# Layer-norm arithmetic of two attentions moved from VectorE to GpSimd, and the side work placed at other heads

## The reference, cut to what matters

```python
ln_out = layernorm(x, ln_s, ln_b)          # (x - m) * rsqrt(v + EPS) * scale + bias
q, k, v = projections                       # self: all of ln_out; cross: k, v of encoder_states
scores = einsum('bhqd,bhkd->bhqk', q, k) / sqrt(HD)      # 16 heads of 32 channels
scores = scores * mask - 10000.0 * (1.0 - mask)
ctx = merge_heads(softmax(scores) @ v)
x = x + ctx @ w_o + b_o
```

## Time and profile before

| what | value |
|---|---|
| median of 3 runs | 4261.32 us (4250.41, 4262.61, 4261.32) |
| profiled execution | 4252.74 us, its span 4250.9 us |
| mean granted TensorE clock | 0.954 of full speed |
| busy, share of the span | PE 88%, DVE 71%, PEld 68%, ACT 48%, POOL 41% |

### The profile page before, as it was taken

The page is one execution under the profiler, slowest core; times in us unless marked ns, Lnnn a source line. Parts: engine busy times, 40 slices in busy tenths (PEclk is TensorE's granted clock), DMA queues, the critical chain, the costliest instruction groups (busy, mean ns, idle before and its releaser), DMA issues. The chain is left out here.

```text
span 4250.9 us, 71399 instructions
## 1 busy us (share of the span) xinstructions
PE 3730.4 (88%) x21636; PEld 2882.3 (68%) x21636; DVE 2998.0 (71%) x6732; ACT 2057.8 (48%) x5384; POOL 1742.2 (41%) x1210
## 2 busy tenths in 40 slices
PE   5998998588888886999999778999999999999976
PEld 4777777477777774899999655666666666666643
DVE  5777777477777775556556338888888878888872
ACT  4777777367777675545545322333333333333322
POOL 2444444144444441000000135666666666666652
PEclk9999999799999997999999889999999999999988
DMA  3434434344444443010010210000000000000000
GB/s 110 104 99 109 104 99 104 96 116 118 104 114 110 122 104 116 30 44 30 30 41 33 73 50 18 24 24 23 24 23 24 23 24 23 24 23 23 23 18 15
DMA packets 146611, 256.58 MB, mean 60 GB/s; under 512 B 27184, under 2 KB 32048, under 8 KB 145424
## 3 DMA queue, kind: packets, MB, share of 16 engines
q1 hardware_dynamic: 146448, 254.49, 22.0%
HBM read 107.62 MB, written 33.55 MB: 33 GB/s over the span
## 5 line engine op out<-in xcount | busy, mean ns | idle before, releaser
L1201 POOL TENSOR_TENSOR c_S<-c_S,c_rT 128x1024 f32<-128x1024 f32 x256 | 558.1, 2180 | 458.4 <-DVE c_S L1479 417.6
L1479 DVE TENSOR_TENSOR_SCAN c_S<-c_wT,c_s,c_vb 128x256 f32<-128x256 f32 x1024 | 709.0, 734 | 45.0 <-issue 2.7
L1474 DVE TENSOR_TENSOR c_vb<-c_kT,c_vb 128x512 f32<-128x512 f32 x512 | 352.4, 688 | 286.4 <-PE c_vb L1645 255.6
L348 POOL TENSOR_TENSOR x_prob<-x_prob,x_rsums 128x512 f32<-128x512 f32 x256 | 275.2, 1075 | 477.7 <-DVE x_rsums L510 477.7
L348 POOL TENSOR_TENSOR s_prob<-s_prob,s_rsums 128x512 f32<-128x512 f32 x256 | 275.2, 1075 | 431.0 <-DVE s_rsums L510 431.0
L1645 PE MATMUL c_vb<-c_vhl,c_spread 128*128 128x512 f32 x512 | 300.4, 597 | 73.6 <-DVE c_S L1479 60.6
L404 ACT ACTIVATE x_prob<-x_t,x_tmin 128x256 f32<-128x256 f32 x512 | 256.4, 502 | 218.3 <-DVE x_tmin L503 218.0
L404 ACT ACTIVATE s_prob<-s_t,s_tmin 128x256 f32<-128x256 f32 x512 | 256.5, 502 | 193.9 <-DVE s_tmin L503 193.6
L862 PE MATMUL b_ps<-b_ln_high,b_w_high 128*128 128x256 f32 x1024 | 290.9, 284 | 14.8 <-DVE b_ln_low L804 14.8
L863 PE MATMUL b_ps<-b_ln_low,b_w_high 128*128 128x256 f32 x1024 | 290.8, 284 | 0.0
L864 PE MATMUL b_ps<-b_ln_high,b_w_low 128*128 128x256 f32 x1024 | 290.8, 284 | 0.0
(11 more groups left out here) (266 smaller groups left out, 10572.4 us busy)
## 6 DMA issues: line engine op xcount, KB each, us to landing
s_stack<-s_parts_qk SPq DMA_DIRECT2D x384, 128.0 KB, 2.4
x_stack<-x_parts_qk SPq DMA_DIRECT2D x384, 128.0 KB, 2.4
s_x_in<-in_x SPq DMA_DIRECT2D x16, 512.0 KB, 3.6
s_xb<-in_x SPq DMA_DIRECT2D x16, 512.0 KB, 4.1
x<-s_x_out SPq DMA_DIRECT2D x16, 512.0 KB, 4.8
x_enc<-in_ctx SPq DMA_DIRECT2D x16, 512.0 KB, 4.4
x_x_in<-x SPq DMA_DIRECT2D x16, 512.0 KB, 3.7
x_xb<-x SPq DMA_DIRECT2D x16, 512.0 KB, 4.1
```

The source lines that it names most:

```text
L348: nc.gpsimd.tensor_tensor(prob[:, h % 4, :, :], prob[:, h % 4, :, :], rsums[:, h, :].unsqueeze(2).to_broadcast([P, TC, T]), ALU.mult).then ...
L1201: nc.gpsimd.tensor_tensor(S[:, n % 4, :, 0:T], S[:, n % 4, :, 0:T], rT[:, par, :, :], ALU.mult).then_inc(z_ready, 1)
L1474: nc.vector.tensor_tensor(pair(vb, i), pair(kT[:, par, :, :], i), pair(vb, i), ALU.mult)
L1479: op = nc.vector.tensor_tensor_scan(S[:, n % 4, c, 1:T + 1], wT[:, par, c, :], vb[:, c, :], s0[:, par, c, n:n + 1], ALU.mult, ALU.add)
```

## The change: what it does

It does four things in both attentions, and nothing in the other two phases.

1. POOL, no longer DVE, forms the normed input: two TENSOR_SCALAR instructions of 128x512 behind the power, at head 3 instead of head 6. DVE's statistics move from head 4 to head 3.
2. POOL, no longer DVE, forms the low parts of lnT0 and lnT1, at head 7 (self) or 6 (cross), behind its product of the head before.
3. The addition to `xb` on POOL moves from head 1 to head 2 (self) or 3 (cross).
4. The side work on PE, ACT and DVE stands at other heads, with one table for each attention.

```diff
@@ -131,9 +131,12 @@
     LT = 3
 
 
-    FILLS = {0: ["k2", "ctx2"], 1: ["q3"], 2: ["k3"], 4: ["ctx3"], 5: ["v0"],
-             6: ["v1"] + (["encT0", "encT1"] if cross else []), 7: ["lnT0", "lnT1", "out0"], 8: ["out1", "ctx0"],
-             9: ["q0"], 10: ["k0"], 11: ["q1"], 12: ["k1", "ctx1"], 15: ["q2"]}
+    SELF_FILLS = {0: ["q3"], 1: ["k2"], 3: ["k3"], 4: ["ctx2", "ctx3", "v0"], 6: ["v1", "lnT0", "lnT1"], 7: ["out0"], 8: ["out1", "ctx0"], 9: ["q0"], 10: ["k0"], 11: ["q1", "k1"], 12: ["ctx1"], 13: ["q2"]}
+    SELF_AT = {"xb": 2, "root": 3, "stats": 3, "low": 7}
+    CROSS_FILLS = {1: ["q3", "k2"], 2: ["ctx2"], 3: ["k3", "ctx3", "v0"], 4: ["v1", "lnT0"], 5: ["encT0", "lnT1"], 6: ["out0"], 7: ["out1"], 8: ["encT1"], 9: ["ctx0", "q0"], 10: ["k0"], 11: ["q1"], 12: ["k1"], 13: ["ctx1", "q2"]}
+    CROSS_AT = {"xb": 3, "root": 3, "stats": 3, "low": 6}
+
+    FILLS, AT = (CROSS_FILLS, CROSS_AT) if cross else (SELF_FILLS, SELF_AT)
     PART = {"attn": ("k2", "q3", "k3", "v0", "v1", "ctx0", "ctx1"), "lag": ("ctx2", "ctx3", "out0", "out1"),
             "front": ("encT0", "encT1", "lnT0", "lnT1", "q0", "k0", "q1", "k1", "q2")}
     PART_OF = {name: part for part, names in PART.items() for name in names}
@@ -195,7 +198,7 @@
         mask_released = sem("mask_released")
         filled = sem("filled")
         emptied = {"act": sem("emptied_act"), "dve": sem("emptied_dve")}
-        stats_ready, rstd_ready, xhat_ready = sem("stats_ready"), sem("rstd_ready"), sem("xhat_ready")
+        stats_ready, xhat_ready = sem("stats_ready"), sem("xhat_ready")
         xb_ready, out_ready = sem("xb_ready"), sem("out_ready")
         weights_loaded = [sem("weights_loaded_0"), sem("weights_loaded_1")]
         weight_high, weight_split = sem("weight_high"), sem("weight_split")
@@ -337,7 +340,7 @@
 
                 def body(k, parts):
                     for n in range(NH):
-                        if n == 1 and "lag" in parts:
+                        if n == AT["xb"] and "lag" in parts:
                             pool.wait_ge(xb_loaded, 16 * k)
                             nc.gpsimd.tensor_tensor(xb[:, :, :], xb[:, :, :],
                                                     row_out[:, :].unsqueeze(1).to_broadcast([P, TC, C]),
@@ -348,10 +351,19 @@
                             nc.gpsimd.tensor_tensor(prob[:, h % 4, :, :], prob[:, h % 4, :, :],
                                                     rsums[:, h, :].unsqueeze(2).to_broadcast([P, TC, T]),
                                                     ALU.mult).then_inc(prob_ready, 1)
-                        if n == 5 and "front" in parts:
+                        if n == AT["root"] and "front" in parts:
                             pool.wait_ge(stats_ready, k + 2)
-                            nc.gpsimd.tensor_tensor(rstd[:, :], ve[:, :], w["neghalf"][:, :],
-                                                    ALU.pow).then_inc(rstd_ready, 1)
+                            nc.gpsimd.tensor_tensor(rstd[:, :], ve[:, :], w["neghalf"][:, :], ALU.pow)
+                            nc.gpsimd.drain()
+                            for tc in range(TC):
+                                op = nc.gpsimd.tensor_scalar(x_in[:, tc, :], x_in[:, tc, :], mv[:, tc, 0:1],
+                                                             rstd[:, tc:tc + 1], ALU.subtract, ALU.mult)
+                            op.then_inc(xhat_ready, 1)
+                        if n == AT["low"] and "front" in parts:
+                            for i in range(2):
+                                pool.wait_ge(emptied["act"], units.emptied(k + 1, f"lnT{i}"))
+                                high, low = [x[:, 2 * i:2 * i + 2, :] for x in ln_parts]
+                                nc.gpsimd.tensor_tensor(low, lnT[:, 2 * i:2 * i + 2, :], high, ALU.subtract).then_inc(ln_split, 1)
 
                 iterations(pool, body)
 
@@ -447,7 +459,7 @@
 
                 def move(k, name, parts):
 
-                    if name in ("v0", "v1"):
+                    if name in ("v0", "v1", "lnT0", "lnT1"):
                         return
                     if PART_OF[name] not in parts:
                         if units.reader(name) == "dve":
@@ -456,11 +468,7 @@
                         return
                     i = int(name[-1])
                     u = ps[:, units.unit(name), :]
-                    if name[:-1] == "lnT":
-                        dve.wait_ge(emptied["act"], units.emptied(k + 1, name))
-                        high, low = [x[:, 2 * i:2 * i + 2, :] for x in ln_parts]
-                        nc.vector.tensor_tensor(low, lnT[:, 2 * i:2 * i + 2, :], high, ALU.subtract).then_inc(ln_split, 1)
-                    elif name[:-1] == "encT":
+                    if name[:-1] == "encT":
                         dve.wait_ge(high_ready, high_done(k, name))
                         high, low = [x[:, 2 * i:2 * i + 2, :] for x in src_parts]
                         nc.vector.tensor_tensor(low, u.rearrange("p (a n) -> p a n", a=2), high,
@@ -508,12 +516,9 @@
                         if ("lag" if n < 1 else "attn") in parts:
                             dve.wait_ge(exp_done, head(kk, h))
                             nc.vector.reciprocal(rsums[:, h, :], psums[:, h, :]).then_inc(rsum_ready, 1)
-                        if n == 4 and "front" in parts:
+                        if n == AT["stats"] and "front" in parts:
                             dve.wait_ge(x_loaded, 16 * k + 32)
                             layernorm_stats(nc, x_in, stats, mv, ve).then_inc(stats_ready, 1)
-                        if n == 6 and "front" in parts:
-                            dve.wait_ge(rstd_ready, k + 2)
-                            layernorm_apply(nc, x_in, mv, rstd, x_in).then_inc(xhat_ready, 1)
                         for name in FILLS.get(n - 1, []):
                             move(k, name, parts)
                     for name in FILLS.get(NH - 1, []):
```

## The result

| | before | after |
|---|---|---|
| median of 12 runs | 4260.73 us (4250.41 to 4271.32) | 4278.57 us (4269.41 to 4283.99) |
| profiled execution's span | 4250.9 us | 4279.8 us |
| ratio after / before | | 1.0041, 95% interval 1.0029 to 1.0053 |

What follows compares the result with a forecast made beforehand. Neither PE nor DVE was full; they took turns waiting for each other. Cross -22, self -5 and the front bodies +4 made -23 us on 4252.7, 4230, given as 4232 us; range 4190 to 4266.

Steps and rivals of the forecast that it cites:

- part 2, "work onto POOL": POOL's new TENSOR_SCALARs: 1.05 us each between bounds of 0.25 and 2.1, adding 4.2 us a turn.
- the 0.3 us wait at head 6: Self: POOL's product of head 3 comes 0.3 us late for PE's transposes at head 6.
- Rival D: POOL becomes the late one if its TENSOR_SCALAR takes 2.1 us: +45 on -23, about 4275 us; chance 0.06.
- the thin stretch: Cross heads 14, 15 and 0 without side work: some 7 us with PE at about a third, then a lower clock.
- the late product: Self: POOL's product of head 3 held up behind the normed input, 0.3 us in the turn's sum.
- the walk: Head-by-head sum of the new order's turn before clock losses: cross 45.8 us, self 44.9 us.
- The stack DMAs were late at heads 0 and 1: Cross: the first stack slots may be 1 us late at heads 0 and 1, where PE can spare it.
- removing 4 us from DVE is worth nothing by itself in self: Heads 6 and 8: DVE waits for PE there anyway, so 4 us less work only makes it wait longer.
- The wait for encT1's low part: Cross: PE's wait for the encoder's low part, 1.04 us before the change, would be gone before out0.
- DVE's 1.93 us for q2: Head 15: DVE idled 1.93 us because q2 came too late; this would be gone.
- signs of being wrong: Cross over 47.5 us at clock 1.00; PE waiting over 1 us for POOL; lower clock in most turns, q3, k2 5 us.
- A drop in two turns of three: Lower clock under q3 and k2 in cross: 2.2 us in two turns of three, 1.5 us a turn.

Runs made afterwards that it cites:

- ts_forms: Changed kernel with four other forms of POOL's normed-input TENSOR_SCALAR, leaving out parts of the layer norm, for durations only; one execution, 4221.7 us.
- norm_dve: Changed kernel with DVE forming the normed input again; POOL keeps the power and low parts, new order stays; 4220.99 us, 0.9917 of the kernel before.
- order_only: norm_dve with the low parts of lnT0 and lnT1 back on DVE too, so the new order alone; 4222.90 us, 0.9917 of the kernel before.
- split_ts: Changed kernel with POOL's second normed-input TENSOR_SCALAR one head later, behind the product of head 3; 4232.89 us, 0.9952 of the kernel before.
- cross_k1_early: norm_dve with k1 of cross-attention one head earlier, at head 11, and ctx1 at head 12; 4226.54 us, 0.9922 of the kernel before.
- lnt0_later: norm_dve with lnT0 of cross-attention behind head 5 instead of 4, q2 at 13; another chip, 0.9937 of the kernel before.
- q2_14_lnt0: norm_dve with cross-attention's lnT0 behind head 5 and q2 behind head 14; another chip, 0.9925 of the kernel before.
- q2_late_lnt0: norm_dve with cross-attention's lnT0 behind head 5 and q2 behind head 15; another chip, 0.9910 of the kernel before.

## Why the prediction was wrong

**The step that failed** is the price in part 2, "work onto POOL": 1.05 us for the TENSOR_SCALAR, "the row of the same size". It measured 2.08, within 0.02 of the upper bound. That turned the 0.3 us wait at head 6 into 2.04 (1.76 in the other turns). The better row was there: the 0.246 us of 64 columns, which the prediction took as a lower bound as it stood, is 1.97 for 512 columns by eight times, 5% from the measurement. It was the same instruction, with constants for the pointers, at an eighth of the size, where the 1.05 was another instruction at the same size. Rival D had the mechanism, the place and the size of the wait ("the product of head 3 is 2.1 us later"), and its 4275 us lies 4 us from the measured median. It had a chance of 0.06, and a reason that was no reason: "even the two-input product takes half of that" compares two different instructions. The range left it out. That D's total fits so well is partly luck: it gives a self turn of 45.35 + 1.7 = 47.05 us, where 47.8 was measured, and a cross turn of 47.3 + 1.3 = 48.6, where 47.7 was measured, and the two errors cancel.

**A second term was left out of D too**: the lower clock after PE's wait, 1.4 us on v1 in every other turn, the difference between 47.1 and 48.5 us. The prediction looked for the clock only behind the thin stretch, and had no term for it behind the wait. ts_forms, with 3.5 us of normed input instead of 4.14, has self turns of 46.0 us; norm_dve has 44.3.

**Right:** the turns of the new order, by their sums more than by their terms. Self without the late product and the clock was given as 44.2 to 45.0 us; norm_dve's turns at a clock of 1.00 take 43.5, so the walk was 0.7 us too long at least. Its turns with the lower clock are 1.8 us longer, where the sum had 0.9 in half of them. The mean is 44.3. Cross was given as 45.8 and 1.5 for the clock, 47.3; it is 47.7. The stack DMAs were late at heads 0 and 1 (1.98 and 0.97 us, given as 1), and q3 and k2 lost 2.1 us. That removing 4 us from DVE is worth nothing by itself in self: order_only takes nothing off DVE and has turns of 44.4 us, norm_dve takes the low parts off it (44.3), split_ts takes all off it (44.6). The wait for encT1's low part and DVE's 1.93 us for q2 are gone. Two of the prediction's own signs of being wrong came: PE waited over 1 us at head 6, and the lower level stood in most turns with q3 and k2 at 5 us.

**Half right:** the clock. A drop in two turns of three was assumed in cross and in half of the self turns; it is in every one. In self with the product on time (norm_dve) it is in about every other.

**Left open:** why cross turns hold to 47.7 or 47.8 us in seven orders (the changed one, norm_dve, split_ts, order_only, cross_k1_early, lnt0_later, q2_14_lnt0), whether PE waits at lnT0, at the stacks or at both. The turns settle on this length from either side: in norm_dve from 47.3 us up to 47.8, in cross_k1_early from 48.1 down to 47.8, each over its first seven turns, while the lower level comes once in every turn. In split_ts a longer wait came with less time at the lower clock, and only a shorter normed input on POOL (ts_forms, 46.1) or q2 at head 15 (47.0, and 47.3 in q2_late_lnt0) left that value. Why ts_forms left it, when norm_dve with no normed input on POOL at all did not, no run shows. That the clock holds it is argued from these runs, not shown by one that sets the clock.

The GpSimd figure of the Trainium skill ("GPSIMD Engine Reference", section "Elementwise — side-by-side cycle accounting", 769 ns for 512 elements) is the best case of a loop and was not reached by any form here: the cheapest took 1511 ns, with one constant. The measurement decides.

## What to carry to other kernels

Where an in-order engine takes on new work, ask first which small product is queued behind it and who waits for that: beside the same work on VectorE (44.3 us a turn), the same 4.1 us on GpSimd cost 3.5 us a turn in one place and 0.3 us with one 1.04 us instruction let through in the middle. An operation that the trace does not show at its size may stand there at another: scale that row by the columns before you borrow from another instruction. Without such a row, both bounds must stand in the range, and the far one is not unlikely because a different instruction is cheap. A change that moves work and reorders it is two changes: here the order alone gave 0.8%, the move alone cost 2.3%.

## What the runs showed of the hardware

GpSimd's TENSOR_SCALAR on 128x512 float32 takes 1.51 us with one constant, 1.93 with two, 1.57 with one pointer and 2.08 with two, all more than the TENSOR_TENSOR product of the probabilities (1.04) and the subtraction that makes the low parts, with its fp32r output (1.29). With two constants 64 columns take 0.246 us, an eighth of 512 within 2%. In self-attention of the kernel before, GpSimd's product took up to 1.41 us, and 1.05 at most in the changed kernel, where VectorE makes neither the normed input nor the low parts. On TensorE the wait of 2.0 us at head 6 was followed by the lower clock in every other turn, which added 1.4 us to it. In cross-attention, taking away PE's wait for the stacks (cross_k1_early) or for lnT0 (lnt0_later) left the turn at 47.8 us and its clock at 0.93.
